# First attention by blocks on two queues, tokens 4p+t in row p, and an FFN routing shared with GpSimd: one Trainium2 core

## The reference

```python
x = x + attn_a(layernorm(x))   # a, xc from two projections to 64 complex numbers
                               # s[t] = a[t] * s[t-1] + a[t] * u[t],  u = inv(V) @ (xc shifted by one)
                               # out = real(V @ s + xc) @ w_out.T
x = x + ffn(layernorm(x))      # 16 experts; each takes its 256 highest of the 4,096 tokens,
                               # gelu(xn @ fc1 + b1) @ fc2 + b2, times its gate, gates divided by their sum
x = x + attn_b(layernorm(x))   # linear attention, 16 heads of 8, running sums over the tokens
x = x + ffn(layernorm(x))      # the same weights
```

## Time and profile before

| | |
|---|---|
| median of 3 runs (lowest, highest) | 764.98 us (763.76, 766.53) |
| profiled execution, and its span from first to last instruction | 773.48 us, 771.7 us |
| busy PE, DVE, POOL, ACT | 434.5, 471.5, 347.9, 208.8 us |
| first attention with its adds | 0 to 191 us |
| first FFN (routing up to 272), reading back | 191 to 376, to 398 us |
| second attention | 398 to 566 us |
| second FFN (routing up to 644), reading back and stores | 566 to 754, to 771.7 us |

### The profile page before, as it was taken

One profiled execution on the slowest core, in us unless ns is written; L12 is line 12 of the kernel. 1 busy time (PEld: TensorE's weight loads), 2 busy tenths in 40 slices (PEclk: granted clock), 3 DMA queues, 4 the chain that ended last, 5 costly groups with the idle time before them and its releaser, 6 DMA issues.

```text
span 771.7 us, 7616 instructions
## 1 busy us (share of the span) xinstructions
PE 434.5 (56%) x2146; PEld 289.0 (37%) x2146; DVE 471.5 (61%) x1205; ACT 208.8 (27%) x511; POOL 347.9 (45%) x330
## 2 busy tenths in 40 slices
PE   4787476008432157778007889888753313887730
PEld 3544344007211056667003334334331102776630
DVE  5475699999777712222066898999967883221211
ACT  2547100000443013223026333323143401232210
POOL 5000790000100066888425877787810004688872
PEclk9999568658855578999558888998976555889975
DMA  4790000000500522333730000000050014233359
GB/s 128 265 400 8 0 0 1 0 0 7 157 0 0 148 52 37 45 45 37 159 79 0 0 1 1 0 1 0 1 163 2 0 47 133 44 45 44 36 84 277
DMA packets 63684, 47.30 MB, mean 61 GB/s; under 512 B 9184, under 2 KB 58976, under 8 KB 62368
## 3 DMA queue, kind: packets, MB, share of 16 engines
q1 hardware_dynamic: 52256, 37.81, 16.1%
q0 software_dynamic: 11392, 9.05, 8.8%
HBM read 26.92 MB, written 19.92 MB: 61 GB/s over the span
## 4 chain that ended last, share of the span: by engine, by line
DVE 24%; POOL 24%; issue 18%; PE 13%; DMA 9%; ACT 5%; SPq 3%; another core or an unknown queue 1%; DVEq 1%; POOLq 0%
POOL acc L431 9%; DVE arena L934 8%; POOL tb L459 8%; DMA acc<-arena,idx 5%; POOL arena L415 4%; DVE tk L939 2%; PE ps L720 2%; DVE arena L939 2%; PE ps L689 2%; DVE tb L969 2%; DMA tab<-tb 2%; PE ps L768 1%; DMA arena<-acc 1%; POOL arena L455 1%
## 5 line engine op out<-in xcount | busy, mean ns | idle before, releaser
L431 POOL DMA_INDIRECT acc<-arena,idx x64 | 101.2, 1581 | 27.6 <-issue 16.2
L934 DVE TENSOR_TENSOR arena<-ps,arena 128x256 f32<-128x256 f32 (+1 forms) x36 | 16.3, 453 | 138.0 <-DMA acc<-arena,idx 115.4
L549 ACT ACTIVATE arena<-ps,b 128x256 f32<-128x256 f32 x128 | 50.1, 474 | 148.1 <-PE ps L820 115.8
L820 PE MATMUL ps<-arena,f1w 128*128 128x256 f32 x256 | 74.5, 442 | 27.7 <-DVE arena L938 23.1
L459 POOL TENSOR_TENSOR tb<-arena 128x512 f32<-128x512 f32 x64 | 80.5, 1271 | 17.0 <-DVE arena L1296 17.0
L867 PE MATMUL ps<-xT,arena 128*128 128x512 f32 x128 | 72.3, 660 | 20.3 <-DVE arena L1296 20.2
L415 POOL DMA_INDIRECT arena<-tab,idx x64 | 62.4, 975 | 41.8 <-DMA tab<-tb 22.9
L830 PE MATMUL ps<-f2w,arena 128*128 128x128 f32 x512 | 68.5, 287 | 7.1 <-issue 7.0
L830 PEld LDWEIGHTS ps<-f2w,arena 128*128 128x128 f32 x512 | 67.4, 203 | 10.7 <-issue 8.1
L820 PEld LDWEIGHTS ps<-arena,f1w 128*128 128x128 f32 x256 | 54.1, 222 | 39.9 <-DVE arena L938 26.9
L934 DVE TENSOR_TENSOR arena<-arena 128x256 f32<-128x256 f32 (+26 forms) x127 | 56.4, 479 | 2.6
(11 more groups left out here) (220 smaller groups left out, 948.1 us busy)
## 6 DMA issues: line engine op xcount, KB each, us to landing
tab<-tb SPq DMA_DIRECT2D x8, 576.0 KB, 5.7
f1w<-in_f1T SPq DMA_DIRECT2D x4, 1024.0 KB, 11.0
f2w<-in_f2T SPq DMA_DIRECT2D x4, 1024.0 KB, 13.0
acc<-tb SPq DMA_DIRECT2D x16, 256.0 KB, 12.1
acc<-xs SPq DMA_DIRECT2D x16, 256.0 KB, 6.3
xs<-acc SPq DMA_DIRECT2D x16, 256.0 KB, 5.5
arena<-acc SPq DMA_DIRECT2D x16, 256.0 KB, 5.4
xs<-in_x SPq DMA_DIRECT2D x8, 256.0 KB, 4.9
```

Of the source, the lines that this page charges most:

```text
L431: pool.indirect_dma_start(out=acc[f][e % 2], out_offset=bass.IndirectOffsetOnAxis(ap=idx[:, i:i + 1], axis=0), in_=yv[:, e % 2, h, :], in_ ...
L549: last = nc.scalar.activation(hT[:, e % 2, t, :], ps[:, 2 * (e % 2) + t // 2, (t % 2) * CAP:(t % 2 + 1) * CAP], ACT.Gelu, bias=b1[:, e, t: ...
L820: last = nc.tensor.matmul(ps[:, 2 * (e % 2) + t // 2, (t % 2) * CAP:(t % 2 + 1) * CAP], f1w[:, e, t * P:(t + 1) * P], xeT[:, e % 2, :], st ...
L934: return nc.vector.tensor_tensor(o, a, b, op)
```

## The change

**Loads.** SP loads four pieces of V's transpose and x of batch 1, ACT four pieces of V and x of batch 0. ACT then makes one root, which loads its table.

**Rows.** Token 4p + t of a group is now in row p of tile t. A row's four tokens are 2 KB in a piece in DRAM (512 bytes each before), for x, the bases, the copies back, and 2,304 bytes for `tab` (576 before, now eight stores instead of four). `xT` stays in the order of the tokens, so ACT writes it with every fourth element, and PE reads columns `[q::4]` in the router's transposes, the way out and the output projection.

**Inverse.** Ten pairs of iterations with constants of their own (`form`, `square`, `apply`) and two single ones (`form`, `apply`): 34 steps where there were 48; eight stand ahead of the first root (five before), twelve ahead of the blocks, six in each block. ACT copies 128 x 256 in `square`. ACT, and not DVE, builds BD and MB.

**Blocks.** All groups are normalised ahead of the loop, into free parts of `lev` and `SS`. ACT copies the projections to SBUF first and squares the copies. POOL makes the first two levels block by block.

**Routing.** POOL adds up the exponentials by halves and makes the product with the reciprocals. The counts come back by SP (three), ACT (three) and POOL (two). The token numbers of the first four experts are made ahead of the others'.

**FFN.** One pair of buffers serves the first FFN. In the second one the base goes to `out`, all experts' rows are added to `out`, each expert behind the landing of the one before, six experts are gathered ahead instead of seven, and the reading back, the sums and the stores are gone.

The diff's core:

```diff
+        PAIRS = (3.9,) * 8 + (3.4, 2.2)
+        SLOPES = (3.9, 3.4, 2.2)
+        N_PAIR, N_LAST = len(PAIRS), 2
+        UNITS = [(i, part) for i in range(N_PAIR) for part in ("form", "square", "apply")]
+        UNITS += [(i, part) for i in range(N_PAIR, N_PAIR + N_LAST) for part in ("form", "apply")]
+
+        AT_ROOT, AT_FIRST, AT_STEP = 8, 12, 6
+
+        BY_BLOCK = 2
...
-        NSP = 6
+        NSP = 3
...
+        def load_x(queue, g):
+
+            b, k = divmod(g, NK)
+            queue.dma_start(xs[:, g * TPG:(g + 1) * TPG, :],
+                            x[b, k * GW:(k + 1) * GW, :].rearrange("(p t) d -> p t d", p=P)).then_inc(x_in[g], 16)
+
         @block.sync
         def _(sp):
-            for t, src in ((RT[0:64, 0:64], vrT), (RT[64:128, 64:128], vrT), (RT[0:64, 64:128], viT), (RT[64:128, 0:64], viT),
-                           (Rm[0:64, 0:64], vr), (Rm[64:128, 64:128], vr), (Rm[0:64, 64:128], vi), (Rm[64:128, 0:64], vi)):
+            for t, src in ((RT[0:64, 0:64], vrT), (RT[64:128, 64:128], vrT), (RT[0:64, 64:128], viT), (RT[64:128, 0:64], viT)):
                 sp.dma_start(t, src).then_inc(inv_in, 16)
-            for g in [b * NK + k for k in range(NK) for b in range(NB)]:
-                b, k = divmod(g, NK)
-                sp.dma_start(xs[:, g * TPG:(g + 1) * TPG, :],
-                             x[b, k * GW:(k + 1) * GW, :].rearrange("(t p) d -> p t d", p=P)).then_inc(x_in[g], 16)
+            for k in range(NK):
+                load_x(sp, NK + k)
...
-            for f in range(2):
-                for g in range(NG):
-                    sp.dma_start(acc[f][1][g * GW:(g + 1) * GW, :].rearrange("(p r) w -> p (r w)", r=TPG), zero
-                                 ).then_inc(zeroed, 16)
+            for g in range(NG):
+                sp.dma_start(acc[1][g * GW:(g + 1) * GW, :].rearrange("(p r) w -> p (r w)", r=TPG), zero
+                             ).then_inc(zeroed, 16)
...
-                    sp.dma_start(acc[f][0][g * GW:(g + 1) * GW, :].rearrange("(t p) w -> p t w", p=P),
+                    sp.dma_start((outf if f else acc[0])[g * GW:(g + 1) * GW, :].rearrange("(p t) w -> p t w", p=P),
                                  xs[:, g * TPG:(g + 1) * TPG, :]).then_inc(base_in, 16)
...
                 for c in range(NSP):
                     spread_counts(sp, f, c, seg_in)
                 sp.wait_ge(tab_ready, f + 1)
-                for q in range(4):
-                    t = slice(8 * q, 8 * q + 8)
-                    sp.dma_start(tab[f][q * 1024:(q + 1) * 1024, :].rearrange("(t p) w -> p t w", p=P), tb[:, t, :]
-                                 ).then_inc(tab_stored, 16)
-                sp.wait_ge(scattered[0], 32 * NE // 2 * (f + 1))
...
-                    sp.dma_start(xs[:, g * TPG:(g + 1) * TPG, :], acc[f][0][g * GW:(g + 1) * GW, :].rearrange("(t p) w -> p t w", p=P)
+                    sp.dma_start(tab[f][g * GW:(g + 1) * GW, :].rearrange("(p t) w -> p t w", p=P),
+                                 tb[:, g * TPG:(g + 1) * TPG, :]).then_inc(tab_stored, 16)
+                if f:
+                    sp.wait_ge(base_in, 16 * NG * 2)
+                    sp.wait_ge(out_scattered, 32 * NE)
+                    return
...
+            for k in range(NK):
+
+                pool.wait_ge(proj_used, k + 1)
+                if k + 1 < NK:
+                    pool.wait_ge(mag_ready, k + 2)
+                pool.wait_ge(transposed, min(2 * (k + 2), NG))
+                A = av[:, :, k * GW:(k + 1) * GW]
+                for i in range(BY_BLOCK):
+                    n = GW >> (i + 1)
+                    B = lev[:, :, lv_at[i + 1] + k * n:lv_at[i + 1] + (k + 1) * n]
+                    level(A, B, n)
+                    pool.wait_ge(lev_ready, k * BY_BLOCK + i + 1)
+                    A = B
+            for lv in range(BY_BLOCK + 1, LEVELS):
+                n = LT >> lv
+                level(lev[:, :, lv_at[lv - 1]:lv_at[lv - 1] + 2 * n], lev[:, :, lv_at[lv]:lv_at[lv] + n], n)
+                pool.wait_ge(lev_ready, level_done(lv))
...
+                pool.wait_ge(exped, f + 1)
+                ex = exs.rearrange("p (t e) -> p t e", e=NE)
+                w = NE // 2
+                G.step(pool.tensor_tensor(exsum[:, :, 0:w], ex[:, :, 0:w], ex[:, :, w:2 * w], ALU.add))
+                while w > 1:
+                    w //= 2
+                    last = pool.tensor_tensor(exsum[:, :, 0:w], exsum[:, :, 0:w], exsum[:, :, w:2 * w], ALU.add)
+                    if w > 1:
+                        G.step(last)
+                last.then_inc(sum_ready, 1)
+                pool.wait_ge(rsum_ready, f + 1)
+                pool.tensor_tensor(ex, ex, rsum.rearrange("p (t e) -> p t e", e=1).to_broadcast([P, NT, NE]), ALU.mult
+                                   ).then_inc(prob_ready, 1)
+
...
-                for c in range(NSP, NCH):
+                for c in range(NSP + NACT, NCH):
                     spread_counts(pool, f, c, seg_in_pool)
...
+                def scatter(e):
+                    pool.wait_ge(y_ready, f * NE + e + 1)
+                    if f:
+                        if e:
+                            pool.wait_ge(out_scattered, 32 * e)
+                    elif e >= 2:
+                        pool.wait_ge(scattered[e % 2], 32 * (e // 2))
                     for h in range(2):
                         i = h * NE + e
-                        pool.indirect_dma_start(out=XE[:, e % RX, h, :], out_offset=None, in_=tab[f],
-                                                in_offset=bass.IndirectOffsetOnAxis(ap=idx[:, i:i + 1], axis=0)
-                                                ).then_inc(xe_in[e % RX], 16)
-
-                for e in range(RX - 1):
-                    gather(e)
+                        pool.indirect_dma_start(out=outf if f else acc[e % 2],
+                                                out_offset=bass.IndirectOffsetOnAxis(ap=idx[:, i:i + 1], axis=0),
+                                                in_=yv[:, e % 2, h, :], in_offset=None, compute_op=ALU.add
+                                                ).then_inc(out_scattered if f else scattered[e % 2], 16)
+
...
+                got = 2 * AHEAD[f]
+                for s in range(got):
+                    gather(s)
...
+                    if f == 0:
+                        for s in range(got, min(got + 2, 2 * NE)):
+                            gather(s)
+                            got += 1
+                        scatter(e)
+                    else:
+                        scatter(e)
+                        for s in range(got, min(got + 2, 2 * NE)):
+                            gather(s)
+                            got += 1
+                if f:
+                    return
...
+            for t, src in ((Rm[0:64, 0:64], vr), (Rm[64:128, 64:128], vr), (Rm[0:64, 64:128], vi), (Rm[64:128, 0:64], vi)):
+                act.dma_start(t, src).then_inc(inv_in, 16)
+            for k in range(NK):
+                load_x(act, k)
+            act.wait_ge(consts, 1)
+            nc.scalar.activation(s_rt[:, 0:1], ident[:, 0:1], ACT.Sqrt)
...
+                nc.scalar.activation(xT[:, g * GW:(g + 1) * GW].rearrange("p (a t) -> p t a", t=TPG), ps[:, 7, :].rearrange("p (t a) -> p t a", t=TPG), ACT.Copy).then_inc(xT_ready, 1)
...
+                for i, raw in enumerate((av[:, :, k * GW:(k + 1) * GW], XC[:, :, 1 + k * GW:1 + (k + 1) * GW])):
+                    act.wait_ge(projected, 2 * k + i + 1)
+                    nc.scalar.activation(raw, ps[:, 2 * i:2 * i + 2, :], ACT.Copy).then_inc(raw_ready, 1)
+                    inverse(at + 2 * i + 1)
+                    if k + 1 < NK:
+                        keep_xT(0, 2 * (k + 1) + i, i * NK + k + 1)
+                    if i == 0 and k >= 1:
+                        roots(k - 1)
+                    act.wait_ge(raw_ready, 2 * k + i + 1)
+                    last = nc.scalar.activation(sq[:, 2 * i:2 * i + 2, :], raw, ACT.Square)
+                    if i == 1:
+                        last.then_inc(squared, 1)
+                    inverse(at + 2 * i + 2)
+                inverse(at + 6)
+            roots(NK - 1)
+            inverse(len(UNITS))
+            act.wait_ge(nw_newT, N_PAIR + N_LAST + 1)
+            lo_, hi_ = slice(0, 64), slice(64, 128)
...
+                act.wait_ge(cnt_stored, 16 * (f + 1))
+                for c in range(NSP, NSP + NACT):
+                    spread_counts(act, f, c, seg_in_act)
...
-                    way_out(n, t, 2, XC[:, 0, at:at + P])
+                    at = n // 2 * GW + 2 * (n % 2) + t
+                    way_out(n, t, 2, XC[:, 0, 1 + at:1 + at + GW - 3:TPG])
...
+            for i, a in enumerate(SLOPES):
+                for j, value in enumerate((2 / a, a - a * a / 4, a / 2)):
+                    V.did(nc.vector.tensor_scalar(cI[:, 3 * j + i, :], ident[:, :], value, None, ALU.mult))
...
+            for g in order[:1]:
+                dve.wait_ge(x_in[g], 16)
+                stats(g)
...
```

(13 more changed lines are left out.)

368 lines of the change are left out of this document (190 added, 178 removed).

## The result

The changed kernel took 755.37 us (749.02 to 757.86, 4 runs) beside 765.75 for the kernel before on the same chip: a ratio of 0.985, 95% interval 0.982 to 0.988. Two more measurements beside the kernel before gave 0.9895 (0.9865 to 0.9924) and 0.982 (0.978 to 0.986). It is faster by 1.0 to 1.8%, clear of the 0.3%, but 22 us above the predicted 733 and outside the range.

A forecast was written before the change was run, and what follows sets the result against it. No engine held a quarter of the chain, so the change was priced stage by stage: terms summed to -31.9 us, a span of 739.8 from 771.70, scaled to 733 us; range 722 to 750.

The forecast's parts named there:

- term 3: Every-fourth-element access by ACT and PE: +1.5 us in the way out, 0.2 an eviction, the rest inside other terms.
- Term 5: Between first FFN and second attention: copies back at 403 instead of 294 GB/s, -4.5 us.
- Term 6: Second FFN: shorter gather burst, chained scatters to out, no reading back or stores behind the last landing, -12.5 us.
- Term 1: First attention up to the last coefficient: later root, block loop of 12.4 us a block, +3.5 us.
- Term 2: Last coefficient to the tree: copies leave DVE, levels made block by block, the hole shrinks, -17.9 us.
- Rival 3: Strides cost the full factor in blocks, routings and way out, 7 us more, 740; chance 0.11.
- Term 4: Each routing, to the first gather: cnt stored later, but fewer pieces read back and quicker tab, -1.0 us, twice.
- rival 5: Row length does nothing: copies back gain nothing, each routing loses 2.1 us, 742; chance 0.06.
- rival 4: Second FFN: the chain of scatters decides; at landings of 6.5 us the time is 773; chance 0.04.

The follow-up runs named there:

- e13: The kernel before, unchanged, profiled a third time: 766.50 us, span 764.6.
- e14: The changed kernel with the old rows put back and all slices contiguous, beside the changed kernel on one chip: 737.49 us, ratio 0.963.
- e6: The changed kernel, but GpSimd starts its levels only when the coefficients of all blocks are done: 763.74 us, ratio 0.9975.
- e16: The changed kernel again, beside e14, e15 and the kernel before on one chip: 753.27 us, ratio 0.982.
- e4: The changed kernel with the sums of the exponentials and their product back on DVE, behind cnt: 759.25 us, ratio 0.980.
- e5: The changed kernel again, beside variants and the kernel before on one chip: 757.08 us, ratio 0.9895.
- e15: The changed kernel with the evictions' loop turned, writing xT in order and reading PSUM with a stride, on e14's chip: 738.19 us, ratio 0.962.
- e1: The changed kernel with the old rows put back and all slices contiguous, first run: 743.10 us, ratio 0.959.
- e9: The changed kernel with in-order evictions, second-attention reciprocals and products tile by tile, and DVE's own sums; order of gathers kept: 731.05 us, ratio 0.954.
- e12: The kernel of e9 in which GpSimd too waits at its end for the landing of all scatters: 732.71 us, ratio 0.956.

## Why the prediction was wrong

The sign was right. The step that failed is the price of the strides: term 3 took less than half of a factor that came in full, and the second attention was given nothing. Two further sizes, terms 5 and 6, were too good. By its own terms, against e13:

- **Term 1** (+3.5, measured -2.5). "one takes 1.4" is right for the old steps, but it was carried over to the new ones: three of those take 2.9 together (ACT's evictions at 14.94 and 17.84), 1.0 each, so eight of them cost little more than the old five, and the root came at 18.11. A block took 11.9 us instead of 12.8, and only 10.7 with contiguous writes (e14: 24.33 to 56.40 for three). (The "six passes" of ACT are five in the kernel; their 5.5 us is the sum of five.) The 18.6 from the last projection on was nearly right: 19.1.
- **Term 2** (-17.9, measured -17.6) was right. For the levels by block e6 shows the reason; the part of the copies and of the inverse's end is argued from the rows. Two small errors cancel: the bits took 5.0 us and not 5.9, the chunks 24.4 and not 23.2.
- **Term 3** is the failure that weighs most. I took "a little under half" of the factor 1.6 of the earlier trace rows because ACT and PE "only write or only load so". ACT's writes paid it in full and more: 1.08 to 0.59 is 1.8, 0.5 us each instead of 0.2; PE's weight loads paid 1.4. Its own +1.5 for the way out came out as measured (+1.5), in part by luck, as the layout alone costs 0.8 there (e16 less e14). Worse, I priced it in the blocks, the routings and the way out and let the second attention "keep its order" at nothing, though it holds eight of these evictions, each on the path, and 64 of PE's products. Layout alone: 5.8 + 0.8 + 2 x 4.2 + 9.7 = 24.7 us of cost, where my terms held about 4. Some 5 of the 8.4 in the routings are the low clock that came with the evictions, which no term had. (The rows of 2 KB give 6 of it back; the 18.7 left are the difference of the two spans, 19.0, 3 more than that of the medians, as the profiled executions lay at opposite sides of theirs.) Rival 3 was the right mechanism, with 0.11 and at a price of 7, because its list has the same hole. The note that I cited (the Trainium skill, SBUF — State Buffer, the cachelines under Door 1) agrees with ACT's 592 and 1,079 ns in these rows, and in direction with PE's loads (237 and 327 ns): the full factor had been the value to take.
- **Term 4** (-1.0 each, measured +3.0 and +2.5). The row length paid as forecast (8.6 against 10.6 us). The evictions cost 4.2 and not 0.5. `cnt` came 2.1 later behind the logits (51.7 us against 49.6; 1.3 in the second routing), about as forecast, and that GpSimd's part would bring nothing held (e4).
- **Term 5** (-4.5, measured -2.1). The direction was right and rival 5 wrong: 313 to 338 GB/s in three profiles of the changed kernel against 284 in e14 at 512 bytes. But in e5 the stage was only 0.3 us shorter than in e13. The size came from stores to DRAM at 403, and copies back did not reach that. The Trainium skill (DMA: Bandwidth & Descriptors, Specifications) gives 512 bytes as the size from which the line rate is had; here 2 KB were still 1.1 to 1.2 times as quick, and the measurement decides.
- **Term 6** (-12.5, measured -3.4). Two mistakes. Its base, 127.2, held 3 us of pause that undisturbed runs of before do not have (124.2). The forecast kept a pause, in the 18.8 to the first scatter, but that took 17.35, so 1.5 of the 3 us was booked as gain and the other 1.5 was expected to stay; scaling the whole sum by 0.991 did not repair that. And "Up to the last landing" was taken for the end: 4.0 us lie behind it, with another 0.6 an expert in the chain of scatters (POOL starts 0.75 us behind a landing; I had 0.1). The scatters' landings stayed at 3.3, so the size that rival 4 needed did not come.

Term 4 and the missing one for the second attention make 15 us of the 20 between -31.9 and -11.5, term 6 makes 9, term 5 makes 2.4, and term 1 gives 6 back: an error of the other sign, without which the miss would have been larger. The range's slow side (to 750) took in each term's end, but not a stage that had been given no term.

## What to carry over

- When a layout changes, list every instruction that writes or loads along it, in all stages, also those whose code "keeps its order"; then ask of each which side of the copy carries the stride. The stride belonged on the side of PSUM: that single turn of a loop was worth 15 us, more than the whole change (10 us).
- Before a wait is booked as gain, take a second profile of the kernel before, on another chip; a profile 1% over the median is a reason to look which rows differ.
- A chain of waits priced "up to the last landing" lacks what the program does at its end, and work that used to hide that (the stores here) no longer does.

## What the runs showed of the hardware

- ACT writing 128 x 512 floats of PSUM to SBUF takes 0.59 us in order, 1.08 with a stride of four elements on the SBUF side, and 0.59 with the stride on the PSUM side. A weight load of 128 x 128 floats took 225 to 259 ns in the second attention, and 327 with every fourth element (e16 and e15).
- Between the end of GpSimd's last instruction and the end of the span lie 5.5 to 5.9 us in four kernels (before, the changed one, e1, e9), and a wait put at GpSimd's end moved the end by 2.0 (e12).
- On one chip, and in the first profile of before, PE, DVE and ACT stood still behind a burst of indirect gathers, so that GpSimd waited up to 4 us for the first y. Four programs showed it there; three of them ran again on another chip, without it. The cause is open.
- The granted clock in the transposes of a routing was 0.70 to 0.86 where an eviction took 0.69 us, and 0.50 to 0.53 in thirteen of fourteen routings where it took 1.09; at the low clock the sixteen products behind them took 3.64 us instead of 1.92. One routing with slow evictions kept 0.78 and was 2.6 us shorter (e4).
